# The row-maximum pass of a one-core attention kernel: a ring of three single banks instead of pairs and singles

## The reference

```python
q, k, v = (split_heads(layernorm(x) @ W) for W in (Wq, Wk, Wv))   # B=4, S=2048, 16 heads of 16
scores  = einsum('bhqd,bhkd->bhqk', q, k) * HEAD ** (-0.5)
scores  = where(causal, scores, -inf)
x = x + einsum('bhqk,bhkd->bhqd', softmax(scores), v) @ Wo + bo
h = layernorm(x)
x = x + int8_matmul(quantised rows of h, quantised columns of rhs) * scales
```

## Time and profile before

| What | us |
|---|---|
| three runs: median (lowest, highest) | 2089.18 (2076.88, 2106.33) |
| the profiled execution, its own time | 2088.25 |
| its span, first to last instruction | 2086.5 |
| PE busy in the span | 1741.6 (83%) |
| DVE busy | 1596.8 (77%) |
| ACT busy | 1267.8 (61%) |
| mean granted TensorE clock, as a share | 0.914 |

### The profile page before, as it was taken

One profiled execution on the slowest core, in us unless ns is written; L12 is line 12 of the kernel. 1 busy time (PEld: TensorE's weight loads), 2 busy tenths in 40 slices (PEclk: granted clock), 3 DMA queues, 4 the chain that ended last, 5 costly groups with the idle time before them and its releaser, 6 DMA issues. The chain is left out here.

```text
span 2086.5 us, 33292 instructions
## 1 busy us (share of the span) xinstructions
PE 1741.6 (83%) x12735; PEld 595.2 (29%) x12735; DVE 1596.8 (77%) x2161; ACT 1267.8 (61%) x1587; POOL 263.6 (13%) x315
## 2 busy tenths in 40 slices
PE   5969767888888888888988888888888888887764
PEld 3646312222222222222222222222222222224442
DVE  5525597888888888888788978887888888504776
ACT  2323103767777777677677767776777677794443
POOL 4000000001110101010100000110101010113443
PEclk9989755999999999999899989998999899998876
DMA  2444100010110101010101010100001010042662
GB/s 83 144 152 128 55 0 11 14 40 27 28 27 28 40 28 39 15 41 14 40 14 40 14 40 25 30 27 27 27 28 38 22 34 20 24 125 72 189 185 90
DMA packets 102448, 105.72 MB, mean 51 GB/s; under 512 B 19092, under 2 KB 85912, under 8 KB 102296
## 3 DMA queue, kind: packets, MB, share of 16 engines
q1 hardware_dynamic: 102296, 103.60, 16.8%
HBM read 60.56 MB, written 42.47 MB: 49 GB/s over the span
## 5 line engine op out<-in xcount | busy, mean ns | idle before, releaser
L748 ACT ACTIVATE prob<-psum 128x1024 f32<-128x1024 f32 (+3 forms) x1280 | 1091.0, 895 | 529.2 <-PE psum L644 523.8
L858 DVE TENSOR_REDUCE pmax<-psum 128x2 f32<-128x1024 f32 (+2 forms) x1264 | 1154.8, 962 | 183.9 <-PE psum L596 110.8
L660 PE MATMUL psum<-prob,V 128*32 128x512 f32 (+3 forms) x5120 | 629.6, 565 | 3.5 <-ACT ust L738 3.3
L644 PE MATMUL psum<-Q,K 50*128 50x512 f16 (+3 forms) x2560 | 580.4, 360 | 12.1 <-ACT prob L748 11.2
L596 PE MATMUL psum<-K,Q 48*128 48x512 f16 x1536 | 397.8, 408 | 156.0 <-DVE pmax L858 146.8
L765 POOL TENSOR_SCALAR_AFFINE_SELECT prob<-prob 128x512 f32<-128x512 f32 x256 | 163.1, 637 | 1699.4 <-ACT prob L748 1699.4
L596 PEld LDWEIGHTS psum<-K,Q 48*128 48x128 f16 x1536 | 97.1, 94 | 656.0 <-DVE pmax L858 492.4
L644 PEld LDWEIGHTS psum<-Q,K 50*128 50x128 f16 x2560 | 157.9, 95 | 103.6 <-ACT prob L748 71.4
L615 PE MATMUL psum<-K,Q 48*128 48x512 f16 (+3 forms) x1024 | 187.0, 323 | 0.0
L610 PE MATMUL psum<-mask,maskid 64*128 64x128 bf16 (+2 forms) x1280 | 147.0, 244 | 46.1 <-DVE pmax L858 34.2
L858 DVE TENSOR_REDUCE pblk<-psum 128x8 f32<-128x1024 f32 (+1 forms) x192 | 159.0, 863 | 28.1 <-PE psum L615 24.3
(11 more groups left out here) (104 smaller groups left out, 720.3 us busy)
## 6 DMA issues: line engine op xcount, KB each, us to landing
unnormalised<-ust SPq DMA_DIRECT2D x64, 256.0 KB, 2.5
xs<-in_L_attn_x SPq DMA_DIRECT2D x16, 512.0 KB, 5.3
q_parts<-part SPq DMA_DIRECT2D x64, 128.0 KB
k_parts<-part SPq DMA_DIRECT2D x64, 128.0 KB
Q<-q_parts SPq DMA_DIRECT2D x128, 64.0 KB, 2.3
K<-k_parts SPq DMA_DIRECT2D x128, 64.0 KB, 2.1
f_us<-unnormalised SPq DMA_DIRECT2D x32, 256.0 KB
f_rs<-inverse_sums SPq DMA_DIRECT2D x32, 256.0 KB
```

The lines of the kernel that those rows point to most:

```text
L644: m = nc.tensor.matmul(PS[:, SB + 2 * pair + half, 0:CH - lo], K[it % 2][rows, pair, kb * P:(kb + 1) * P], Q[it % 2][rows, pair, c * CH + ...
L660: m = nc.tensor.matmul(PS[32 * h:32 * h + 32, UB, lo:CH], V[:, it // NG * NT + kb, col:col + 32], prob[(it * NSTEP + k) % PRING][:, h, 0:C ...
L748: nc.scalar.activation(prob[g % PRING][:, 2 * pair:2 * pair + 2, 0:n], PS[:, SB + 2 * pair:SB + 2 * pair + 2, 0:n], ACT.Exp, scale=by).the ...
L858: nc.vector.tensor_reduce(to, of, axis=AX.X, op=ALU.max).then_inc(mx_free, 1)
```

## The change

Four things change in `attend`. A max turn is one half of one tile in one bank; turns go round banks 5, 6 and 7, and turn n waits for turn n - 3. That gives 137 turns per iteration with the tail. The values of a step are issued in two halves of the columns, the first after the scores of pair 0, the second after those of pair 1. Where turns stand in PE's order is no longer a share of the columns: `place_turns` walks through the program with a fixed duration for each kind of work and puts a turn ahead of a piece of work if its bank would be free by then. PE waits once per chunk and iteration for Q and K, instead of at every turn. SP's `max_rows` of the next iteration goes from `ci == 1` to `ci == 2`, the third chunk.

```diff
-SPREAD = 35
-EARLY = 5
...
+def order_of_turns():
...
+    for it in range(ITS):
+        turns += [(it, kind, half) for kind in KINDS for half in range(2)]
+        tail.append(len(turns))
+        turns.append((it, None, 0))
+    return turns, tail
...
+SLOTS = 4
+RING = 2
+MRING = 3
...
+def place_turns():
...
+    hop, land, mask = 0.12, 0.27, 0.85
...
+    def turn_free():
+        it, kind, half = TURNS[n]
+        at = turn_at[n - MRING] + hop if n >= MRING else 0.0
+        for c in chunks_of(kind) if kind and it >= 2 else ():
+            if (it - 2, NCH - 1 - c) not in staged:
+                return None
+            at = max(at, staged[it - 2, NCH - 1 - c] + 6.0)
+        return at if kind else turn_at[n - 1] + 1.6
+
+    def issue_turns(limit):
...
+            if free is None or (limit is not None and max(pe, free) > max(pe, limit)):
+                return
+            it, kind, half = TURNS[n]
+            pe = max(pe, free) + (0.08 if kind is None else 0.23 if kind[0] == "off" else 0.35)
+            vec = max(vec, pe + land) + (2.6 if kind is None else 0.6)
...
+            h = slot // 2
+            ready = max(tail_at[it] + 4.0, exp_at[g - 1, h] + hop if g else 0.0)
+            issue_turns(ready)
+            upto[g, slot] = n
...
-                    if ci == 1 and more:
+                    if ci == 2 and more:
                         max_rows(it + 1)
...
             def max_turn(n):
-                it, kind, halves = TURNS[n]
-                if n >= 2:
-                    pe.wait_ge(mx_free, n - 1)
-                at = banks(n, halves)
+                it, kind, half = TURNS[n]
+                if n >= MRING:
+                    pe.wait_ge(mx_free, n - MRING + 1)
+                at = MB + n % MRING
...
-            def values(it, k):
+            def values(it, k, second):
+
                 c, kb = STEPS[k]
                 lo = step_cols(c, kb)
+                mid = (lo + CH) // 2
...
+                if not second:
+                    if kb == 0 and it * NCH + ci >= 1:
+                        pe.wait_ge(u_staged, it * NCH + ci)
+                    pe.wait_ge(exp_done, it * NS + 2 * k + 2)
+                    if kb >= TPC * c:
+                        pe.wait_ge(masked, it * NT + ci * TPC + kb - TPC * c + 1)
+                cols = slice(mid, CH) if second else slice(lo, mid)
                 for h in range(G):
                     col = VS * ((it % NG) * G + h)
...
+                if second:
+                    m.then_inc(p_free, 1)
...
                 for k in range(NSTEP):
...
+                    for slot in range(SLOTS):
+                        for n in range(issued, UPTO.get((g, slot), issued)):
+                            max_turn(n)
+                        issued = UPTO.get((g, slot), issued)
+                        if slot in (1, 3):
+                            if g >= LAG:
+                                values((g - LAG) // NSTEP, (g - LAG) % NSTEP, slot == 3)
+                            continue
+                        if k == 0 and slot == 0:
+                            pe.wait_ge(mrows_in, (it + 1) * MROWS)
+                        scores(it, k, slot // 2)
```

More of the change, by code:

```diff
@@ L73, in chunks_of @@
     return {kind[1]} if kind[0] == "diag" else {kind[2] // TPC, kind[3]}
[L76 to L98, removed]
+def order_of_turns():
+    turns, tail = [], []
@@ L590, in _ @@
         def _(pe):
+            arrived = [set() for _ in range(ITS)]
             def max_bank(it, kind, half, bank):
@@ L683, in ffn_weight @@
                 i.then_inc(wpe, 1)
-            cols = [CH - step_cols(*s) for s in STEPS]
-            for n in range(BEGIN[0]):
-                max_turn(n)
+            issued = 0
             for it in range(ITS):
-                more = it + 1 < ITS
-                if not more:
+                if it + 1 == ITS:
                     pe.wait_ge(mx_free, len(TURNS))
-                pe.wait_ge(mrows_in, (it + 1) * MROWS)
-                if not more:
                     for c in range(NCH):
@@ L696, in _ @@
                         pe.wait_ge(chunk_in[it % 2][c], (it // 2 + 1) * (16 * LOADS))
-                at = BEGIN[it]
                 for k in range(NSTEP):
-                    if not more and k in (2, 20):
+                    g = it * NSTEP + k
+                    if it + 1 == ITS and k in (2, 20):
                         ffn_weight(k // 20)
[L701 to L724, removed]
@@ L725, in _ @@
             for k in range(NSTEP - LAG, NSTEP):
-                values(ITS - 1, k)
+                for second in (False, True):
+                    values(ITS - 1, k, second)
         @block.scalar
@@ L831, in max_turn @@
             def max_turn(n):
-                it, kind, halves = TURNS[n]
-                at = banks(n, halves)
+                it, kind, half = TURNS[n]
+                at = MB + n % MRING
                 if kind is None:
-                    first = min(at.values())
                     combine(it)
@@ L861, in _ @@
             dve.wait_ge(init, 1)
-            for n in range(BEGIN[0]):
+            for n, (it, kind, _) in enumerate(TURNS):
+                if it >= 2 and n == (TAIL[it] + TAIL[it - 1]) // 2:
+                    invert(it - 2)
                 max_turn(n)
[L864 to L868, removed]
-                middle = (BEGIN[it] + TAIL[it + 1]) // 2
-                for n in range(BEGIN[it], BEGIN[it + 1]):
-                    if n == middle and it >= 1:
-                        invert(it - 1)
-                    max_turn(n)
+            invert(ITS - 2)
+            ffn_weight()
 def finish(nc, x_t, u_d, r_d, out_t, PS, identb, eps, F):
```

98 lines of the change are left out of this document (60 added, 38 removed).

## The result

The changed kernel takes 2163.4 us (median of 4 runs, 2157.67 to 2174.42); the kernel before, measured again beside it, 2090.78. The ratio is 1.0347, 95% interval 1.0294 to 1.0400: **slower by 3.5%**, where 2140 us and a range of 2045 to 2215 had been forecast. The profiled execution took 2157.67, 69.4 more than that of before.

What follows compares the result with a forecast made beforehand. PE was to become the bound: 89.6 us of need plus 4.0 of waits, 5.9 of boundary stall and 2.3 of clock gave 101.8 us per iteration against 98.0, so +52 us in all, 2140 us, range 2045 to 2215.

Steps and rivals of the forecast that it cites:

- What bounds the kernel before: PE and DVE, each near 87% busy, wait for each other; 16.5 us of waits per iteration can be won.
- PE's need, 89.6 us: PE's work per iteration without waits: 78.2 us plus 11.4 for halved values, more entries into values and more turn slots.
- PE becomes the bound: After the change PE's need of 89.6 us per iteration exceeds DVE's 84.6.
- Remaining waits, 4.0: PE's waits left per iteration: 2.4 us for ACT's copy, the rest steps with few turns and banks; ends 2 and 8.
- The moved DMAs, 5.9 us at 14 boundaries: At iteration boundaries PE stalls for maxima's writes queued on SP behind a store and eight loads; about 2 at the last.
- The clock, 2.3 us: Loss per iteration from the granted clock lowered after each boundary stall; ends 1.5 and 5.5.
- The sum: Per iteration 93.6 + 5.9 + 2.3 = 101.8 us against 98.0, +53 us over 14; with both ends +52, 2140 us.
- The start: First max pass, alone at clock 0.50, takes 94 us before; it gives back 7 us.
- the last iteration: Values in halves but no turns, ACT busy 61 of 70 us: +2 us, ends 0 and 6.
- the first: First iteration, partly at the low clock, with its boundary: +4 us.
- Worse: Every stall brings the long clock loss, 5.5 us, and bank waits grow 3 us: 2227 us; chance 0.15.
- fast rival: DVE becomes the bound if 256-column halves cost 0.50 us and entry nothing: 92.7 per iteration, 2013 us; chance 0.09.

Runs made afterwards that it cites:

- trace with halves: Kernel before, with every group of values split into two column halves, back to back at the old place: 2050.9 us, ratio 0.9829.
- whole values: Early writes, with each step's values in one piece again after the scores of pair 1: 2034.8 us, ratio 0.9723.
- pairs: Early writes, with each first half of a tile moved to its second half's place: 2018.0 us, ratio 0.9640.
- Early writes: Changed kernel with `max_rows` back at `ci == 1`, the second chunk: 1988.8 us, ratio 0.9484; repeated on another chip 1986.9 us, 0.9525.
- filled stall: Changed kernel, writes still late, with 24 pairs of spare matmuls ahead of the wait for them at 14 boundaries: 2105.9 us, ratio 1.0021.
- rows ahead: Changed kernel with the maxima's writes still at the third chunk but ahead of its store and loads: 2080.8 us, ratio 0.9936.

## Why the prediction was right

The number, the direction and the path by which the loss came were right. In the sum the clock was far too small and the waits were too large, and these errors partly cancelled.

- **What bounds the kernel before: right.** Waits between PE and DVE of some 16 us are what the change could win. Without its late writes it wins them in part: 94.7 for a clean period before, 90.8 to 92.9 after.
- **PE's need, 89.6 us: right in size, wrong in what it was laid on.** Halves of 512 columns do take 0.57 to the next start in the changed kernel (TensorE's timeline):

```profile
1071.88 0.64 PE L709 MATMUL psum<-prob,V 128*32 128x256 f32 x8
1072.45 0.39 PE L642 MATMUL psum<-K,Q 48*128 48x512 f16 x1
```

  The prediction took the 0.58 beside 1.00 in the earlier trace rows as the cost of halving. Two halves in a row cost 1.00, so the 0.14 more of two separate ones is the cost of leaving the values and coming back. The rule in the Trainium skill ("TensorE: Matmul & The Clock Gate", Back-to-back issue gap) makes halving nearly free. The trace with halves agrees, 1.00 for sixteen matmuls as for eight; the changed kernel, where the halves stand apart, does not. The forecast was right to go by the row. "PE becomes the bound" held only for this order: taking 10 us from PE by whole values or by pairs made it slower, adding 8.8 cost 5.1. The two engines and the three banks bind together. (The groups of turns given ahead of the prediction, 88 of one, 20 of two and 4 of three, hold 140 turns, not 136, because turns of two iterations stand in those steps; by the table the tiles of one iteration take 112 to 115 slots, where 116 were counted.)
- **Remaining waits, 4.0: too many.** Early writes have 91.7 where 93.6 had been summed. Of the 4.0, 2.4 were to be the first values of a chunk waiting for ACT's copy; in the waits of the changed kernel above that is 6.4 us in the whole execution, 0.4 per iteration. In one iteration of early writes (889 to 981) PE is recorded waiting for 0.9 us in all and busy for 90.7 of 92. A wait that is shorter than the matmul still in flight does not show in such rows, so these are lower bounds.
- **The moved DMAs, 5.9 us at 14 boundaries: right.** The writes were landed 7.9 us behind the copy, as worked out, and PE's wait totals 82.1 us over 15 boundaries against 14 x 5.9 + 2 = 85, 5.7 each and 2.5 at the last. Undoing that one line turned a loss of 3.5% into a gain of 5%. (The tail turn is six steps earlier than before, at step 29 for 35, and eleven ahead of the iteration's end; the prediction's "eleven steps earlier" is the latter.)
- **The clock, 2.3 us: the mis-sized term.** It cost 5.0 by the filled stall alone, and the low stretch at twelve of the thirteen boundaries between the first copy and the last was 20 to 27 us, where the longest of before was 14. The prediction's own rows spoke for more: a mean period of 98.0 beside a clean one of 94.7 is a loss of 3.3 us in the kernel *before*, and the long loss is 7.0 over the clean period, not the 5.5 over its neighbour. A kernel with a stall at every boundary was given less than one without any had already lost.
- **The sum.** Early writes 91.8 + recorded wait 5.5 leave 6.4 of the measured 103.7 for the clock. By the price of the filled stall, 0.29, the 19 us more of low clock than in early writes cost 5.5; by that of the kernel before, 0.43 for the 16 or so outside the stall, 7. Forecast were 101.8: waits 2 too many, stall 0.4 too much, clock nearly 4 too little. That the first two took back more than half of the third is luck. The start gave 8.8 instead of 7, the last iteration cost 2.7 instead of 2, the first gained 2.3 where 4 had been added.
- **Rivals.** "Worse", with the long clock loss at each boundary, described the clock rightly, but its extra waits for banks did not come (6 us in all), which kept the time under its 2227. The fast rival's condition, 0.50 us for a half and nothing on entry, did not hold with the halves apart (0.57). That the kernel without its stall reaches 1989 is another matter: the rival's own sum kept the stall.

## What to carry to other kernels

When a wait is relaxed by moving an issue in a DMA queue, count everything that is now ahead of it on that queue from the moment the queue is released: that the maxima were ready eleven steps ahead of their need was worth nothing behind eight loads of 0.47 us. A stall of TensorE is to be priced with the clock behind it: here 5.7 us idle cost another 5 to 7, and 1.5 idle nearly 5. Cutting a run of matmuls in two was free (1.00 us either way) as long as nothing came between; coming back to it once more cost 0.14. And where two engines passed three banks between them, smaller pieces (0.57 us against 0.60 that DVE takes for a bank) did better than less work in larger ones (91.8 against 95.2 us per period).

## What had not been expected

Splitting values in the kernel before made it 1.7% faster though its clean periods did not move (94.9 beside 94.7 us): the gain is in the granted clock alone, 0.98 for 0.96. Why the split keeps the clock up is not shown. And the level of 0.5 outlasted its cause. In the changed kernel the low stretches began in the stall and, at twelve of thirteen boundaries, went on for 15 to 23 us behind it, with PE recorded busy nearly all the time once it had started again (20.2 of 24 us in the row above, the stall's last 4 included). With stalls of 1.5 us, in the kernel with the rows ahead, most low stretches lasted 17 to 20 us.
